# The end of an expert layer: a second sum added by accumulating transfers, and the residual by VectorE instead of GpSimd

## The reference, cut to what matters

```python
xn = _layernorm(x)
x = x + L0_attn(xn) + L0_experts(xn)    # windowed attention; 64 experts, top 8, at most 128 tokens each
xn = _layernorm(x)
x = x + L1_attn(xn) + L1_experts(xn)    # linear attention of 16 heads; 8 experts, top 1, and a shared one
```

## Time and profile before

| | |
|---|---|
| median of 3 runs | 1352.87 us (1349.44 to 1354.07) |
| profiled execution, its own time | 1343.85 us |
| its span, first to last instruction | 1342.1 us |
| TensorE busy | 1266.8 us (94%) |
| VectorE, GpSimd, ScalarE busy | 686.2, 681.7, 520.2 us (51%, 51%, 39%) |
| TensorE's granted clock, mean | 0.976 of full speed |

### The profile page before, as it was taken

One profiled execution on the slowest core, in us unless ns is written; L12 is line 12 of the kernel. 1 busy time (PEld: TensorE's weight loads), 2 busy tenths in 40 slices (PEclk: granted clock), 3 DMA queues, 4 the chain that ended last, 5 costly groups with the idle time before them and its releaser, 6 DMA issues. The chain is left out here.

```text
span 1342.1 us, 20324 instructions
## 1 busy us (share of the span) xinstructions
PE 1266.8 (94%) x7210; PEld 1026.4 (76%) x7245; DVE 686.2 (51%) x1374; ACT 520.2 (39%) x1123; POOL 681.7 (51%) x535
## 2 busy tenths in 40 slices
PE   6589999999879998999999999999999998999998
PEld 5468888888658887888788888888888884666655
DVE  6996555555866578665654335434343342222223
ACT  4345566666465333334233343333433322011110
POOL 3536877775503465666765656556565550000013
PEclk9589999999999998999999999999999998999999
DMA  9603888885405220222121112211111107511213
GB/s 321 195 1 88 180 182 191 178 175 107 165 1 168 67 68 25 66 72 64 61 66 56 52 36 67 63 52 51 36 52 48 36 14 280 184 48 44 64 47 114
DMA packets 99204, 126.99 MB, mean 95 GB/s; under 512 B 11713, under 2 KB 84033, under 8 KB 98977
## 3 DMA queue, kind: packets, MB, share of 16 engines
q1 hardware_dynamic: 84176, 99.59, 23.5%
q0 software_dynamic: 14928, 26.10, 9.9%
HBM read 97.70 MB, written 27.95 MB: 94 GB/s over the span
## 5 line engine op out<-in xcount | busy, mean ns | idle before, releaser
L1528 PE MATMUL a_p_p<-a_xr,a_wr 128*128 128x512 f32 x1152 | 308.6, 403 | 2.4 <-DVE g_x L2078 2.4
L1528 PEld LDWEIGHTS a_p_p<-a_xr,a_wr 128*128 128x128 f32 x1152 | 206.6, 189 | 42.5 <-DVE g_x L2078 3.1
L1846 POOL TENSOR_TENSOR a_sqsum<-a_sqsum,a_sq 128x512 f32<-128x512 f32 x60 | 77.8, 1296 | 232.5 <-ACT a_sq L1731 232.5
L1814 POOL TENSOR_TENSOR a_wr<-g_hold,a_wr 128x768 fp32r<-128x768 f32 x63 | 122.3, 1941 | 20.1 <-DVE a_wr L1878 20.1
L1914 DVE SCALAR_TENSOR_TENSOR a_gated<-a_th,a_p_o 128x512 f32<-128x512 f32 x64 | 44.0, 688 | 159.0 <-ACT a_sq L1731 159.0
L409 POOL DMA_INDIRECT acc<-l_ye,g_slot_token x64 | 102.1, 1595 | 33.6 <-issue 14.7
L1848 POOL TENSOR_TENSOR a_gr<-a_gated,a_gr 128x512 fp32r<-128x512 f32 x64 | 97.7, 1527 | 23.8 <-DVE a_gr L1918 23.8
L1541 PE MATMUL a_p_p<-a_wvr,a_xr 128*128 128x512 f32 x384 | 108.9, 421 | 0.6 <-DVE a_xr L1872 0.6
L1155 POOL DMA_DIRECT2D out<-e_ye x23 | 12.5, 544 | 178.7 <-DVE e_ye L1304 178.7
L1599 PE MATMUL a_p_w<-a_gr,l_wo_r 128*128 128x512 f32 x384 | 100.9, 398 | 2.3 <-POOL a_gr L1848 2.3
L1583 PE MATMUL a_p_o<-a_sc,a_v 128*128 128x128 f32 x512 | 89.8, 278 | 6.7 <-DVE a_sc L1894 6.7
(11 more groups left out here) (273 smaller groups left out, 2735.6 us busy)
## 6 DMA issues: line engine op xcount, KB each, us to landing
g_hold<-in_Wqkg SPq DMA_DIRECT2D x64, 384.0 KB, 3.2
g_hold<-in_gate_up SPq DMA_DIRECT2D x64, 192.0 KB
g_hold<-in_Wv SPq DMA_DIRECT2D x16, 512.0 KB, 4.8
e_up<-in_gate_up SPq DMA_DIRECT2D x8, 1024.0 KB, 14.1
l_down<-in_down SPq DMA_DIRECT2D x64, 96.0 KB
acc<-l_zero SPq DMA_DIRECT2D x2, 2176.0 KB, 11.7
l_lists<-acc SPq DMA_DIRECT2D x8, 512.0 KB, 4.9
e_down<-in_down SPq DMA_DIRECT2D x8, 512.0 KB, 12.2
```

The source lines that it names most:

```text
L1528: mm = pe.matmul(dst[:, :], wr[n % 2][:, wp, kk, c * P:(c + 1) * P], xr[n // H1 % 2][:, xp, kk, :], start=(kk, xp, wp) == (0, 0, 0), stop= ...
L1814: pool.tensor_tensor(wr[n % 2][:, 1, :, :], w[n % 2], wr[n % 2][:, 0, :, :], ALU.subtract).then_inc(w_parts, 1)
L1846: pool.tensor_tensor(sqsum[b % 2][:, :], sqsum[b % 2][:, :], sq[a % 2][:, :], ALU.add).then_inc(summed, 1)
```

## The change

One table's part is loaded by SyncE as before, but all four parts now have a buffer of their own, and none waits for `combined`. The other table's part is added to it by an accumulating transfer, DRAM to SBUF, that GpSimd starts when the load has landed (`part_in[c]`); its landing is `sum_in[c]`. GpSimd does no arithmetic any more at the layer's end. VectorE adds each part to x itself (`combine`), at the steps 59, 60, 61 and 66. The result is the same sum.

```diff
@@ -147,6 +147,7 @@
     PICK0, LISTS, TICK0 = -5, 12, 15
     TAKEN, IS_TAKEN = -3.0e38, -1.0e38
     TICKS = E0 + 2
+    COMBINES = tuple(range(STEPS - 5, STEPS - 2))
     STATS1 = (STEPS - 3, STEPS - 1, STEPS + 1)
     DECAYS = tuple(range(STEPS - 6, STEPS - 2))
...
         queue = lists[:, 3, :].rearrange("p (t n) -> p t n", t=NT // 2)
-        part = [[lists[:, 2 * s + i, :].rearrange("p (t d) -> p t d", t=TPB) for i in range(2)] for s in range(2)]
+        part = [lists[:, c, :].rearrange("p (t d) -> p t d", t=TPB) for c in range(TPB)]
         stats1 = m.sb("stats1", [P, NT - 1, 6])
...
-            def parts(c):
-                if c >= 2:
-                    sp.wait_ge(combined, c - 1)
-                for i in range(2):
-                    acc = g["acc"][i][c * SEQ:(c + 1) * SEQ, :].rearrange("(t p) d -> p t d", p=P)
-                    sp.dma_start(part[c % 2][i], acc).then_inc(part_in[c], 16)
-
             for s in range(YR):
                 sp.wait_ge(summed[s], 16 * (E0 // YR))
-            for c in range(2):
-                parts(c)
+            for c in range(TPB):
+                acc = g["acc"][0][c * SEQ:(c + 1) * SEQ, :].rearrange("(t p) d -> p t d", p=P)
+                sp.dma_start(part[c], acc).then_inc(part_in[c], 16)
             sp.dma_start(g["wv"], wv(io["Wv1"][0:D, :])).then_inc(next_in, 16)
             for h in range(2):
                 sp.dma_start(g["w"][h], wv(io["Wqkg1"][h * D:(h + 1) * D, :])).then_inc(next_in, 16)
-            for c in range(2, TPB):
-                parts(c)
...
-            pool.wait_ge(biased, NT)
-            pool.wait_ge(added, 3 * TPB)
+            for s in range(YR):
+                pool.wait_ge(summed[s], 16 * (E0 // YR))
             for c in range(TPB):
-                at = slice(TPB * c, TPB * (c + 1))
-                pool.wait_ge(part_in[c], 32)
-                pool.tensor_tensor(part[c % 2][0], part[c % 2][0], part[c % 2][1], ALU.add).then_inc(joined, 1)
-                if c < TPB - 1:
-                    pool.wait_ge(joined, c + 1)
-                    pool.tensor_tensor(g["x"][:, at, :], g["x"][:, at, :], part[c % 2][0], ALU.add).then_inc(combined, 1)
+                pool.wait_ge(part_in[c], 16)
+                acc = g["acc"][1][c * SEQ:(c + 1) * SEQ, :].rearrange("(t p) d -> p t d", p=P)
+                pool.dma_start(part[c], acc, accum_op=ALU.add).then_inc(sum_in[c], 16)
...
             def statistics1(c, tiles):
-                if c < TPB - 1:
-                    dve.wait_ge(combined, c + 1)
+                dve.wait_ge(combined, c + 1)
                 first = 2 * c
...
-            def combine_last():
-                at = slice(NT - TPB, NT)
-                dve.wait_ge(joined, TPB)
-                dve.wait_ge(added, NT - 1)
-                dve.tensor_tensor(g["x"][:, at, :], g["x"][:, at, :], part[(TPB - 1) % 2][0], ALU.add).then_inc(combined, 1)
-                dve.wait_ge(combined, TPB)
-                statistics1(TPB - 1, range(NT - TPB, NT - 1))
+            def combine(c):
+                at = slice(TPB * c, TPB * (c + 1))
+                dve.wait_ge(sum_in[c], 16)
+                dve.wait_ge(biased, NT)
+                dve.wait_ge(added, min(TPB * (c + 1), NT - 1))
+                dve.tensor_tensor(g["x"][:, at, :], g["x"][:, at, :], part[c], ALU.add).then_inc(combined, 1)
 
...
                     dve.tensor_scalar(minus_slope[:, :], slope[:, :], -1.0, None, ALU.mult).then_inc(slope_ready, 1)
+                if n in COMBINES:
+                    combine(COMBINES.index(n))
                 if n in STATS1:
                     c = STATS1.index(n)
                     statistics1(c, range(TPB * c, TPB * (c + 1)))
                 if n == LAST - 8:
-                    combine_last()
+                    combine(TPB - 1)
+                    statistics1(TPB - 1, range(NT - TPB, NT - 1))
                 if n == LAST - 6:
```

More of the change, by code:

```diff
@@ L246, in layer0 @@
                  "ex_in_psum", "exT_ready", "h_in_psum", "th_ready", "silu_ready", "hT_ready", "ye_in_psum", "ye_ready",
-                 "slopes_in", "slope_ready", "decays_done", "next_in", "joined", "combined", "stats1_done", "var1_ready",
+                 "slopes_in", "slope_ready", "decays_done", "next_in", "combined", "stats1_done", "var1_ready",
                  "std1_ready", "rstd1_ready")
@@ L257, in layer0 @@
          ex_in_psum, exT_ready, h_in_psum, th_ready, silu_ready, hT_ready, ye_in_psum, ye_ready,
-         slopes_in, slope_ready, decays_done, next_in, joined, combined, stats1_done, var1_ready,
+         slopes_in, slope_ready, decays_done, next_in, combined, stats1_done, var1_ready,
          std1_ready, rstd1_ready) = (m.sem(n) for n in names)
         part_in = [m.sem(f"part_in{c}") for c in range(TPB)]
+        sum_in = [m.sem(f"sum_in{c}") for c in range(TPB)]
         x_in = [m.sem(f"x_in{c}") for c in range(BATCH)]
```

## The result

Four executions of the changed kernel had a median of 1343.78 us (1342.98 to 1345.0), four of the kernel before 1353.15 us (1349.44 to 1354.07). The ratio is 0.9937, with a 95% interval of 0.9916 to 0.9957. Two repeats, on two different chips and against other runs of before, gave 0.9952 (0.9937 to 0.9967) and 0.9956 (0.9943 to 0.9969). So the change makes the kernel about 0.5% faster, some 6 to 8 us. The kernel before, run against itself, gave 1.0004 (0.9993 to 1.0014).

What follows compares the result with a forecast made beforehand. TensorE was busy 94% of the span, so only its lost time could be won. Terms -6.97 + 0 + 1.22 + 0 = -5.75 us took 1352.87 to 1347.1 us; forecast band 1345.9 to 1348.7, eight-in-ten range 1344.0 to 1354.5.

Steps and rivals of the forecast that it cites:

- Removed: seven GpSimd additions: Stretch between the twelfth and thirteenth out-projection sums: without GpSimd's additions it loses 6.97 us, from 18.85 to 11.88.
- the term for the clock: Same stretch: TensorE's matmuls after its pause, 3.43 us at the lower clock, take 1.84 at full clock, 1.59 us gained.
- The lower bound of 4.84 us: Least gain in that stretch, 18.85 less the 14.01 us of the stretch before, which has one projection more.
- The first two cost 0: VectorE's additions at steps 59 and 60 are covered by existing waits; 2.44 us if the cover were gone.
- C: Rival, chance 0.12: all three added VectorE additions are exposed, -3.3 us, giving 1349.6 us.
- The third costs its whole 1.22 us: VectorE's addition between the out-projection sum at 381.39 us and the first statistics delays everything behind it by 1.22 us.
- VectorE has no pause: From the third addition to `l_y` of tile 14 (387.05 us), VectorE has no idle time to absorb the 1.22 us.
- The transfers cost 0: The four accumulating transfers into SBUF land before VectorE's additions need them, costing 0 us.
- some 5 us: Assumed time of one accumulating transfer of 512 KB, that of the plain load of the same bytes.
- A: Rival, chance 0.12: transfers late at the waits for `sum_in[2]` and `sum_in[3]`, 22.3 us, giving 1369.4 us.
- the bound of 17.6 us: Upper estimate for one accumulating transfer: four times the 4.4 us of a scatter accumulating 128 rows.
- B: Rival, chance 0.08: GpSimd's transfer instructions hold VectorE as its additions did, or TensorE's pause has another cause; 1354.1 us.

Runs made afterwards that it cites:

- The run without pauses between the additions: Changed kernel plus seven GpSimd additions nobody waits for, with two different inputs, each waiting only for the one before the last; second stretch 18.83 us.

## Why the prediction was right

**The forecast** was -5.75 us, from 1352.87 to 1347.1; the stretches give -6.26 us, inside its band of -7.0 to -4.2, and the ratios 6 to 8.5 us. The first ratio, 1344.3 us, lies below that band (1345.9 to 1348.7) and just inside the wider range. The direction, the mechanism and the signs were right, but for one: the barrier came at 399.5 us and not at 394, since this execution reached the tail 6.2 us later, which has nothing to do with the change.

**"Removed: seven GpSimd additions", 6.97 us.** Measured 7.26 (18.85 to 11.59). TensorE was idle for 5.38 us of the 18.85 and for nothing of the 11.59, which is exactly the 4.80 and the 0.58. Its busy time fell from 13.47 to 11.59, by 1.88 us, where the term for the clock had 1.59; that term, taken over 3.43 us alone, was 0.29 too small. The run without pauses between the additions showed that the additions alone make the 7.3 us. The lower bound of 4.84 us, from the stretch before, was far too careful.

**"The first two cost 0".** Measured 0.03 us (12.84 to 12.87). The cover was where it was said to be: TensorE's wait for ScalarE, which was 1.43 us, shrank by 1.00 us, VectorE's before the sum from 3.54 to 1.29. C, all three exposed, did not come.

**"The third costs its whole 1.22 us".** It cost 0.94 (9.58 to 10.52). Two things were overlooked. An instruction starts before the row of the last one ends: the statistics start 1.14 us behind the addition (380.69 to 381.83). And "VectorE has no pause" was not quite true: the maxima of step 63 and the reciprocal stood a tenth of a us behind what was ahead of them; these pauses, 0.2 us together, went.

**The transfers cost 0.** Right, but "some 5 us" for one was mis-sized as the time of a transfer, and "all in by 360" was 4 us too early: issue to landing was 10.6 to 14.2 us, with all four under way together, and the last landed at 364.0. As a rate it holds: from the first issue (345.15) to the last landing they took 18.9 us, 4.7 each. The loads were all in within 8.8 us. The Trainium skill, in "Collectives: The Full Stack", section "The bandwidth ceiling: the fold count and why AG ≠ RS ≠ AR", has half the rate for additions in the transfer engines. Over the whole the ratio here is 2.1, but layer 1's weights were under way beside the additions until 355.9 us; from one landing to the next it was 2.8 us on average against 1.7 for the loads, so 1.7 times. No run had either alone. GpSimd's instruction took 1.3 to 1.5 us, not 2.2.

**A**, the late transfers: the last of the four had landed by 364.0 us, 9.8 us ahead of the first addition, and additions six steps earlier still didn't wait. It was far from deciding; the bound of 17.6 us, four times a scatter, was too high. But layer 1's weights, said to be done before 350, landed at 355.9 us. **B** fell with the rows: `l_diag` had 0.42 to 0.43 us throughout, and the four VectorE instructions of the projection that ran beside the transfer instructions (347.0 to 348.6) took as long as without them.

## What to carry to other kernels

Read an instruction's length at two places of the same kernel before looking for what it waits for: a product that takes 0.43 us in one stretch and 1.5 us in another isn't late, it is held, and the engine that holds it is the one whose rows end just ahead of it. In this kernel GpSimd's additions cost most where small VectorE products stood ahead of what TensorE waited for. Moved to transfers they cost nothing, because each had landed before it was used; with the first use 11.1 us behind the first issue that was still so, by 0.9 us. And an addition put into a pause of its engine was free, where the same one between a sum and its statistics cost 0.94 of its 1.22 us.

## What was not expected of the hardware

VectorE's products were not slowed by GpSimd's additions but held to their end. In the six profiles with such additions, 37 products with both inputs in SBUF began while one ran. Of 36 the ones of 128x256 ended 0.28 to 0.29 us behind the end of the addition and those of 128x64 0.08 us behind it, whatever their start; the last one began 0.09 us ahead of the end and took its usual 0.43 us. VectorE's instructions with an input in PSUM kept their length beside them. So the 1.00 us of a product beside additions of one buffer to itself and the 1.46 to 1.50 beside those of two different inputs don't show different holding: the first additions took 1.95 us, the second 2.44, and each product waited for what was left of one. In the same way a pause of a tenth of a us between GpSimd's additions was worth 2.9 us (15.96 against 18.83), as far as the traces tell because it let a small product of 0.2 us begin that otherwise stood for 2.4.
